# Cross-attention with routed experts on one core: the order of input loads, output weights and expert matrices on one DMA queue

## The chip, the core and the metric

One core of a Trainium2 chip runs the whole kernel. The metric is the device time of one execution in microseconds (us). TensorE is called PE in the profile, its weight loads PEld, VectorE DVE, ScalarE ACT, GpSimd POOL, and SyncE, which here only issues DMAs, SP.

## The reference, cut to what matters

There are 32 records of 128 tokens with 256 channels (`x`), each with a context of the same shape (`ctx_1024`).

```python
def _L0_xattn_ref(q, k, v, Wq, bq, Wk, bk, Wv, bv, Wd, bd):   # 16 heads of 16
    query = (q @ Wq.T + bq).reshape(B, -1, H, D)
    key_p = (k @ Wk.T + bk).reshape(B, -1, H, D)
    value = (v @ Wv.T + bv).reshape(B, -1, H, D)
    logits = jnp.einsum('bsid,bsjd->bsij', query, key_p) / jnp.sqrt(jnp.float32(D))
    attn = jax.nn.softmax(logits, axis=-1)          # heads attend to heads, per token
    out = jnp.einsum('bsij,bsjd->bsid', attn, value)
    out = jnp.transpose(out, (0, 2, 1, 3)).reshape(B, -1, O)
    return out @ Wd.T + bd

x = x + _L0_xattn_ref(_layernorm(x, axis=-1), ctx_1024, ctx_1024, ...)
x = x + _L0_ffn_ref(_layernorm(x, axis=-1), ...)
# ffn: gates = softmax(x_red @ wg_n.T) over 8 experts, idx = argmax, scores = max;
#      o = scores * (gelu(x @ W1[idx] + b1[idx]) @ W2[idx] + b2[idx])
```

## The kernel before, in words

**Attention.** A loop over steps t = 0 to 41 runs on every engine; it is a software pipeline written out by hand. In step t, TensorE projects record a = t (`tensor_project`, lines 921, 924 and 1013: key, value, query and gate columns), computes the logits of record t - 6 (line 933), turns the attention of record t - 7 (line 1024), multiplies record w = t - 8 with the output weights (line 977, `wd`), and computes the values of record t - 7 (line 944). In the first 8 steps the projection stands first in the step, from step 8 on it stands behind `wd`. For its first seven steps TensorE also does three idle transposes at the end (`fill`).

**The round trip.** The heads of a token have to be spread over partitions. So two records at a time, keys, queries and values (`qkv`, 768 KB) are stored to a scratch tensor in HBM (line 280) and loaded back in another order (`ql`, two DMAs of 384 KB, line 289). POOL masks what came back into `kx` (line 393) and ACT copies it into `pad` (line 817), both for record z = t - 5.

**Inputs.** `x` comes in pairs of records (256 KB, line 252) into a ring of 14 slots. ACT takes the moments of record t + 2 in step t (`scalar_ahead`, lines 770 and 773); behind them on ACT stand the moments of the attention's result and the copy `oT` (line 837), which `wd` of the next step reads. The transposed inputs `xc` (x and context, 512 KB for two records, line 258) go to a ring of XC = 4 slots in `r1`; POOL permutes the context of record t + 1 in step t (`pool_context`, line 356), TensorE reads both.

**SP's order.** SP issues nearly all DMAs, in program order, on one queue (`sync_attention`). In an odd step t: wait until the records t - 1 and t are ready (`qad`), store them, load `xc` of t + 3; a row store (`sync_row`, line 272); wait until the store has landed and the buffer `ql` is free, issue the two `ql` loads, load `x` of t + 5. In every step also a row store, and the expert matrices that `MATRIX_AT` puts there (16 of 512 KB: eight W1, eight W2; first at step 22, last at step 35). From step 32 on there are four parts of `b2`. `sync_inputs`, ahead of the loop, issues `xc` and `x` of records 2 and 3, then the output weights and bias (`sync_setup_output`: 768 KB in four DMAs), then `x` of 4 and 5.

**Output weights.** `tensor_gate` (lines 1031 and 1034) folds the gate columns into the output weights. It needs `Wd` and `bd_col` and stands behind the projection of record 1. POOL adds the output bias to `x` of record t - 2 (line 402).

**Experts.** While attention still runs, the first 20 records are routed (`vector_early`, steps 27 to 34, on DVE). From step 34 on, slots of 128 tokens gathered by expert go through two matrix products (lines 1086 and 1116). The first slot needs all eight W1 at step 35, the first product with W2 comes in step 37 and needs all eight W2.

Of the kernel before, what the change touches and what calls it, by code (L numbers as in the profile page):

```python
# [4 lines left out]
P = 128  # L5
C = 256
NH = 16
HD = C // NH
NT = 32
# [9 lines left out]
EXT = C + NL  # L19
# [9 lines left out]
NG_ = NH  # L29
W3 = 3 * HD  # L30
XR = 14
XC = 4
CR = 5
RB = 6
YR = 4
# [12 lines left out]
ROUTE = R1 + 7  # L48
SLOTS_AT = {t: (t - FIRST,) for t in range(FIRST, LAST + 1)}
NEXT = LAST + 1 - FIRST  # L50
MATRIX_AT = (22, 24, 26, 27, 28, 29, 30, 31, 32, 32, 33, 33, 34, 34, 35, 35)
B2_IN = 32
B2_PARTS = 4
SHARE = 1
# [1 line left out]
SELR = NH2 + 2  # L56
PIECES = (("oh_a", 1), ("rv_a", 5), ("rv_a", 10), ("rv_a", 13), ("texp_a", 1), ("selk_a", 1), ("taken_a", 1))

SEMS = ("ld_xx ld_cc ld_x0 ld_x1 ld_x2 ld_c0 ld_c1 st_q0 st_q1 ld_q0 ld_q1 st_r0 st_r1 st_r2 st_r3 st_r4 ld_wq ld_wkv ld_wd ld_wo ld_g ld_gr ld_gt ld_b ld_bd "
        "ld_bc ld_w1 ld_w2 ld_b2 filled ident iotas const cp mask4 pad0 nmax gpow ctr0 ctr gmm gate gx gxs "  # L60
        "wqs wTq gsq nr2 wide qq kv kvad qad xb kx pad qk mx lsub exp sm rsm norm tr_a ax0 ax pvo oT wd x2 nb gm gsub "
        "scaled score nm0 va0 va1 ve rs oh cnt rv selr selp selk invmm texp idg ids ig isc yo yb "
# [4 lines left out]
def live(t):  # L67
    return 0 <= t < NT
# [6 lines left out]
def build(nc, x, xc, wkvT, wqT, wdT, Wd, bkvq, bd, bd_col, w_redT, wgT_in, wg, W1b, W2, b2, out):  # L75
# [7 lines left out]
    with es:  # L83
        def sb(name, shape, dt=f32):
            return es.enter_context(nc.sbuf_tensor(name, shape, dt))
# [43 lines left out]
        rsm = sb("rsm", [P, NH])  # L129
        oT = sb("oT", [P, KC, P])  # L130
        cat = [sb(f"cat{k}", [P, ROW + 1]) for k in range(CR)]
        junk = sb("junk", [P, 2, C])
        nm = sb("nm", [P, 1])
        va = sb("va", [P, 2])
        ve = sb("ve", [P, 2])
# [25 lines left out]
        nr2, nrm, nri = (sb(n, [P, NE]) for n in ("nr2", "nrm", "nri"))  # L161
        warm = sb("warm", [P, 2])
        r0 = sb("r0", [P, 3800])[:, :]
        r1 = sb("r1", [P, 2 * W1W + C])[:, :]
        xcT = r1[:, 0:XC * 4 * P].rearrange("p (n a c) -> p n a c", n=XC, a=4)

        oh = sb("oh", [P, NT, NE], bf16)
# [67 lines left out]
        def sync_setup_output(eng):  # L235
            eng.dma_start(wst, Wd.rearrange("(a p) c -> p a c", p=P)).then_inc(S["ld_wo"], 16)
            eng.dma_start(wD[:, :, 0:C], wdT).then_inc(S["ld_wd"], 16)
            eng.dma_start(bdb[:, 0:C], bd.rearrange("(o n) -> o n", o=1).broadcast_to((P, C))).then_inc(S["ld_bd"], 16)
            eng.dma_start(bdm, bd_col).then_inc(S["ld_bc"], 16)
# [14 lines left out]
        def sync_xc(eng, c):  # L254
            if c < NT:
                if c >= XC:
                    eng.wait_ge(S["qq"], c - XC + 2)
                eng.dma_start(xcT[:, c % XC:c % XC + 2, :, :], xc[c // 2]).then_inc(S[f"ld_c{c // 2 % 2}"], 16)

        def sync_inputs(eng):  # L260
            eng.wait_ge(S["ld_xx"], 16)
            sync_xc(eng, 2)
            sync_x(eng, 2)
            eng.wait_ge(S["ld_x0"], 16)
            sync_setup_output(eng)
            sync_x(eng, 4)

        def sync_row(eng, g):
# [5 lines left out]
        def sync_attention(eng):  # L274
            sync_inputs(eng)
            for t in range(LAST + 2):
                p = t // 2
                if live(t) and t % 2 == 1:
                    eng.wait_ge(S["qad"], t + 1)
                    eng.dma_start(qkv_scr[p], qkv[p % 2][:, :, :, :]).then_inc(S[f"st_q{p % 2}"], 16)  # L280
                    sync_xc(eng, t + 3)
                sync_row(eng, t - 10)
                if live(t) and t % 2 == 1:
                    eng.wait_ge(S[f"st_q{p % 2}"], (p // 2 + 1) * 16)
                    if p > 1:
                        eng.wait_ge(S["kx"], t - 3)
                        eng.wait_ge(S["pad"], t - 3)
                    for h in range(2):
                        eng.dma_start(ql[p % 2][64 * h:64 * (h + 1), :, :, :],
                                      qkv_scr[p].rearrange("(h c g) x w d -> h x c g (w d)", h=2, c=NC_)[h]  # L290
                                      ).then_inc(S[f"ld_q{p % 2}"], 16)
                    sync_x(eng, t + 5)
                for m in range(2 * NE):
                    if MATRIX_AT[m] == t:
                        expert(eng, m)
                m = t - B2_IN
                if 0 <= m < B2_PARTS:
                    if m == 0:
                        eng.wait_ge(S["gxs"], 1)
                    h = NE * C // B2_PARTS  # L300
                    eng.dma_start(b2b[:, m * h:(m + 1) * h], b2.rearrange("e c -> (e c)").rearrange("(o n) -> o n", o=1)
                                  [:, m * h:(m + 1) * h].broadcast_to((P, h))).then_inc(S["ld_b2"], 16)
# [44 lines left out]
        def pool_context(eng, a):  # L347
            if live(a):
                if a == 0:
                    eng.wait_ge(S["ld_cc"], 16)  # L350
                else:
                    eng.wait_ge(S[f"ld_c{a // 2 % 2}"], (a // 4 + 1) * 16)
                if a > 1:
                    eng.wait_ge(S["kv"], a - 1)
                for k in range(KC):
                    i_ = eng.tensor_copy(cp[a % 2][:, k, :].rearrange("p (e c h g) -> p e c h g", e=2, c=NC_, h=2),
                                         xcT[:, a % XC, KC + k, :].rearrange("p (h c e g) -> p e c h g", e=2, c=NC_, h=2))
                i_.then_inc(S["cp"], 1)

        def pool_attention(eng):  # L360
            for t in range(-1, LAST + 1):
                n, v, w, d, z = t + 1, t - 2, t - 8, t - 9, t - 5
                if t == -1:
                    pool_norm(eng)
                    pool_context(eng, 0)
# [172 lines left out]
        def vector_attention(eng):  # L538
            for t in range(LAST + 1):
                a, s0, s1, w = t, t - 6, t - 7, t - 8  # L540
                if t < 7:
                    vector_kv(eng, a)
                    vector_q(eng, a)
                if a == 1:
                    eng.wait_ge(S["gx"], 1)
                    eng.wait_ge(S["ld_bd"], 16)
                    eng.tensor_copy(bdb[:, C:EXT], bY[:, 304:304 + NL])
                    eng.tensor_copy(wD[:, :, C:EXT], bY[:, 320:320 + KC * NL].rearrange("p (a e) -> p a e", a=KC)
                                    ).then_inc(S["gxs"], 1)
# [12 lines left out]
                if live(w):  # L562
# [7 lines left out]
                    if w > 0:  # L570
                        eng.wait_ge(S["gsub"], w)
                    eng.tensor_reduce(gm[:, :], cat[w % CR][:, C:C + NE], AX, ALU.max,
                                      negate=True).then_inc(S["gm"], 1)
                if live(a) and t >= 7:
                    vector_kv(eng, a)
                if ROUTE <= t < ROUTE + 7:
                    vector_early(eng, t - ROUTE)
                if live(a) and t >= 7:
                    vector_q(eng, a)
                if live(s0) and t >= STEADY:  # L580
                    normed(eng, s0)
# [184 lines left out]
        def moments(eng, k, w, in_):  # L766
            if k + (0, 10)[w] > 0:
                eng.wait_ge(S["rs"], k + (0, 10)[w])
            if w == 0:
                eng.activation(junk[:, 0, :], in_, ACT.Identity, scale=-1.0 / C,  # L770
                               accum_out=nm[:, :]).then_inc(S["nm0"], 1)
                eng.wait_ge(S["nm0"], k + 1)
            eng.activation(junk[:, w, :], in_, ACT.Square, bias=nm[:, :] if w == 0 else cat[k % CR][:, EXT - 1:EXT],
                           accum_out=va[:, 1 - w:2 - w]).then_inc(S[f"va{w}"], 1)

        def scalar_ahead(eng, t):
# [136 lines left out]
        def tensor_kv(eng, a):  # L913
            if a > 0:
                eng.wait_ge(S["kvad"], a)
                eng.wait_ge(S[f"ld_c{a // 2 % 2}"], (a // 4 + 1) * 16)
            else:
                eng.wait_ge(S["ld_wkv"], 16)
                eng.wait_ge(S["ld_cc"], 16)
            for k in range(KC):  # L920
                eng.matmul(bKV[:, 0:C], xcT[:, a % XC, KC + k, :], wT[:, k, 0:C], start=(k == 0), stop=(k == KC - 1))  # L921
            eng.wait_ge(S["cp"], a + 1)
            for k in range(KC):
                i_ = eng.matmul(bKV[:, C:2 * C], cp[a % 2][:, k, :], wT[:, k, C:2 * C], start=(k == 0),  # L924
                                stop=(k == KC - 1))
            i_.then_inc(S["kv"], 1)
# [23 lines left out]
        def tensor_attention(eng):  # L950
            for t in range(LAST + 1):
                a, s0, s1, w = t, t - 6, t - 7, t - 8
                if t < 8:
                    tensor_project(eng, a)
                if live(s0):
                    eng.wait_ge(S["kx"], s0 + 1)
# [12 lines left out]
                if live(w):  # L969
# [6 lines left out]
                    for k in range(KC):  # L976
                        i_ = eng.matmul(bY[:, 0:EXT], oT[:, k, :], wD[:, k, :], start=(k == 0), stop=(k == KC - 1))  # L977
                    i_.then_inc(S["wd"], 1)
                if live(a) and t >= 8:
                    tensor_project(eng, a)  # L980
                if live(s1):
                    eng.wait_ge(S["ax"], s1 + 1)
# [13 lines left out]
                for s in slots:  # L996
                    if s != 1:
                        tensor_rows(eng, s)
                if t < 7:
                    fill(eng, 3, bA)  # L1000
                if t == NT + 8:
                    tensor_counts(eng)

        def tensor_project(eng, a):
            tensor_kv(eng, a)
            if a > 0:
                eng.wait_ge(S["qad"], a)
            else:
                tensor_weights(eng)
                eng.wait_ge(S["gate"], 1)  # L1010
                eng.wait_ge(S["wTq"], 1)
            for k in range(KC):
                i_ = eng.matmul(bQ[:, 0:EXT], xcT[:, a % XC, k, :], wT[:, k, 2 * C:3 * C + NL], start=(k == 0),  # L1013
                                stop=(k == KC - 1))
            i_.then_inc(S["qq"], 1)
            if a == 1:
                tensor_gate(eng)

        def tensor_turn(eng, t, s1):
# [194 lines left out]
```

## Time and profile before

| | us |
|---|---|
| median of 3 runs (374.09 to 376.0) | 374.12 |
| the profiled execution's own time | 376.52 |
| its span | 374.7 |
| PE busy | 339.7 (91%) |
| DVE busy | 255.8 (68%) |
| POOL busy | 275.0 (73%) |
| ACT busy | 203.7 (54%) |
| DMA moved | 63.90 MB |

The profile cuts the span into 40 slices of 9.4 us. The slices up to 206 us are the attention; the rest is the experts' slots, in which TensorE is busy nearly throughout. Times below are microseconds from the span's start.

### The profile page before, as it was taken

What the parts mean: (1) busy time and instruction counts of PE and PEld (TensorE: products, weight loads), DVE (VectorE), ACT (ScalarE), POOL (GpSimd) and SP (SyncE); (2) the same over time, 40 slices, a digit from 0 to 9 for tenths busy, and PEclk for the clock granted to TensorE, in tenths of its full rate; (3) what the DMA queues carried; (4) which work ended last, traced back from release to release, by engine and by line L of the source; (5) the groups of instructions that cost most, each with busy time, mean ns of one, the idle gap of its engine ahead of it and who ended that gap; (6) DMA issues with size and microseconds to landing.
All of it is one profiled execution on the core that took longest, in us unless ns stands there. A gap on an engine that the chain in (4) does not pass through costs nothing.

```text
span 374.7 us, 11126 instructions
## 1 busy us (share of the span) xinstructions
PE 339.7 (91%) x3755; PEld 290.5 (78%) x3755; DVE 255.8 (68%) x629; ACT 203.7 (54%) x625; POOL 275.0 (73%) x539
## 2 busy tenths in 40 slices
PE   7898599999999998895767997899999999999994
PEld 6786488888878776674645785789999999999993
DVE  6343788989888885899777656784565556565552
ACT  2334668877787866676663646612443434343431
POOL 4758858987889876777978377672777777778763
PEclk9999699999999999899588999997999999999999
DMA  6899989999999999989798011410122222222210
GB/s 230 268 266 270 225 189 241 253 264 265 247 275 282 293 221 256 299 268 270 189 383 309 16 43 59 132 59 27 62 72 69 75 62 77 62 74 60 62 48 0
DMA packets 55414, 63.90 MB, mean 171 GB/s; under 512 B 36558, under 2 KB 45919, under 8 KB 55360
## 3 DMA queue, kind: packets, MB, share of 16 engines
q1 hardware_dynamic: 50832, 52.78, 49.8%
q0 software_dynamic: 3744, 9.55, 8.5%
q10 hardware_dynamic: 784, 0.87, 0.7%
q8 instruction: 31, 0.51, 0.6%
q14 instruction: 23, 0.19, 0.2%
HBM read 42.02 MB, written 22.09 MB: 171 GB/s over the span
## 4 chain that ended last, share of the span: by engine, by line
PE 61%; DMA 13%; DVE 10%; issue 6%; ACT 5%; POOL 3%; SPq 1%; ACTq 1%; DVEq 1%; POOLq 0%
PE bQ L1116 17%; PE bKV L1086 9%; PE bL L1086 9%; DMA xt<-in_x 7%; PE bY L977 5%; PE bKV L921 3%; PE bKV L924 3%; PE bO L944 3%; PE bQ L1013 3%; DMA qkv_scr<-qkv 3%; PE bL L933 3%; PE bT L1098 2%; DMA r<-row_scr,ig 2%; ACT pad L817 1%; PE bA L1024 1%
## 5 line engine op out<-in xcount | busy, mean ns | idle before, releaser
L1116 PE MATMUL bQ<-w,wA 128*128 x312 | 75.0, 384 | 3.0 <-DVE r L756 2.3
L1116 PEld LDWEIGHTS bQ<-w,wA 128*128 128x128 f32 x312 | 56.8, 192 | 10.6 <-issue 4.4
L393 POOL TENSOR_TENSOR x<-ql,mask 128x1024 f32<-128x1024 f32 x32 | 60.6, 1892 | 0.4 <-DVE texp L638 0.4
L423 POOL DMA_INDIRECT out<-r,isc x39 | 40.8, 1046 | 21.7 <-issue 13.9
L446 POOL DMA_INDIRECT r<-row_scr,ig x39 | 41.8, 1071 | 6.1 <-issue 2.2
L884 ACT ACTIVATE wA<-bL,r 128x128 f32<-128x128 f32 x76 | 21.7, 368 | 40.8 <-PE bL L1086 40.8
L884 ACT ACTIVATE wA<-bKV,r 128x128 f32<-128x128 f32 x80 | 22.8, 367 | 35.2 <-PE bKV L1086 35.2
L1086 PEld LDWEIGHTS bKV<-wA,r 128*128 128x128 f32 x320 | 38.5, 192 | 3.6 <-issue 1.8
L1086 PE MATMUL bKV<-wA,r 128*128 128x128 f32 x320 | 39.4, 276 | 2.0 <-DVE wA L745 2.0
L977 PE MATMUL bY<-wD,oT 128*128 128x265 f32 x128 | 39.7, 437 | 1.2 <-ACT oT L837 1.1
L817 ACT ACTIVATE pad<-ql 64x512 f32<-64x512 f32 x64 | 39.8, 622 | 0.4
L1086 PEld LDWEIGHTS bL<-wA,r 128*128 128x128 f32 x304 | 38.4, 199 | 1.6 <-ACT wA L884 0.6
L1086 PE MATMUL bL<-wA,r 128*128 128x128 f32 x304 | 38.8, 283 | 0.0
L756 DVE TENSOR_TENSOR r<-bQ,b2b 128x256 f32<-128x256 f32 x39 | 16.5, 424 | 32.4 <-PE bQ L1116 32.4
L736 DVE TENSOR_SCALAR r<-w1b 128x1028 f32 x39 | 28.5, 732 | 12.9 <-issue 11.6
L921 PE MATMUL bKV<-wA,r 128*128 128x256 f32 x128 | 33.5, 384 | 1.4 <-DMA r<-in_xc 0.9
L944 PEld LDWEIGHTS bO<-ax,pad 128*32 128x32 f32 x1024 | 16.9, 115 | 22.9 <-ACT ax L863 13.7
L1013 PE MATMUL bQ<-wA,r 128*128 128x265 f32 x128 | 33.9, 387 | 0.3 <-DVE wA L479 0.3
L373 POOL TENSOR_TENSOR cat<-ve,half 128x2 f32<-128x2 f32 x42 | 30.8, 733 | 3.5
L924 PE MATMUL bKV<-wA,cp 128*128 128x256 f32 x128 | 33.0, 380 | 0.0
L808 ACT ACTIVATE bX<-bL 128x256 f32<-128x256 f32 x32 | 11.8, 368 | 37.4 <-DVE bL L554 37.4
L944 PE MATMUL bO<-ax,pad 128*32 128x64 f32 x1024 | 22.3, 231 | 10.4 <-ACT ax L863 10.4
(179 smaller groups left out, 694.0 us busy)
## 6 DMA issues: line engine op xcount, KB each, us to landing
qkv_scr<-qkv SPq DMA_DIRECT2D x16, 768.0 KB, 5.1
ql<-qkv_scr SPq DMA_DIRECT2D x32, 384.0 KB, 5.6
r<-in_xc SPq DMA_DIRECT2D x15, 512.0 KB
row_scr<-cat SPq DMA_DIRECT2D x32, 134.0 KB, 5.6
w1b<-in_W1b SPq DMA_DIRECT2D x8, 514.0 KB, 6.0
w<-in_W SPq DMA_DIRECT2D x8, 512.0 KB, 9.7
xt<-in_x SPq DMA_DIRECT2D x15, 256.0 KB, 6.2
b2b<-in_b SPq DMA_DIRECT2D x4, 256.0 KB, 10.9
```

The lines of the kernel that those rows point to most:

```text
L393: eng.tensor_tensor(quarter(kx[:, z % 2, :]), spread(ql[z // 2 % 2][:, :, z % 2, 0:HD]), mask_k, ALU.mult).then_inc(S["kx"], 1)
L423: eng.indirect_dma_start(out, bass.IndirectOffsetOnAxis(ap=isc[k][:, :], axis=0), yo[k], None, bounds_check=NTOK - 1, oob_is_err=False).th ...
L446: eng.indirect_dma_start(gr[k], None, row_scr[0:R1 * P] if a < S1 else row_scr, bass.IndirectOffsetOnAxis(ap=ig[k][:, :], axis=0)).then_in ...
L817: i_ = eng.activation(pad[n, z % 3, :].rearrange("p (k g h d) -> p k g h d", k=2, g=NG_, h=2) [:, :, :, h, :], ql[z // 2 % 2][n, :, z % 2, ...
L884: i_ = eng.activation(hT[a % 2][:, k, :], bH[a % 2][:, k * P:(k + 1) * P], ACT.Gelu, bias=w1s[a % 2][:, KC * HID + k:KC * HID + k + 1])
L921: eng.matmul(bKV[:, 0:C], xcT[:, a % XC, KC + k, :], wT[:, k, 0:C], start=(k == 0), stop=(k == KC - 1))
L924: i_ = eng.matmul(bKV[:, C:2 * C], cp[a % 2][:, k, :], wT[:, k, C:2 * C], start=(k == 0), stop=(k == KC - 1))
L944: i_ = eng.matmul(out_[32 * r:32 * (r + 1), m * P + q * 64:m * P + (q + 1) * 64], stat[:, 32 * g:32 * (g + 1)], moving[:, (8 * m + 2 * r + ...
L977: i_ = eng.matmul(bY[:, 0:EXT], oT[:, k, :], wD[:, k, :], start=(k == 0), stop=(k == KC - 1))
L1013: i_ = eng.matmul(bQ[:, 0:EXT], xcT[:, a % XC, k, :], wT[:, k, 2 * C:3 * C + NL], start=(k == 0), stop=(k == KC - 1))
L1086: i_ = eng.matmul(bH[a % 2][:, k * P:(k + 1) * P], w1s[a % 2][:, c * HID + k * P:c * HID + (k + 1) * P], gT[a % 2][:, c, :], start=(c == 0 ...
L1116: i_ = eng.matmul(bQ[:, 0:C], hT[b % 2][:, k, :], w2[:, bass.ds(eb * (KH * C) + k * C, C)], start=(k == 0), stop=(k == KH - 1))
```

## The change

The first rows of `MATRIX_AT` move from step 22 to step 27 and the matrices come closer together. `XC` becomes 6, with a third semaphore for the loads; from step 5 on `xc` of t + 5 is loaded behind the `ql` loads and `x`, where `xc` of t + 3 was loaded ahead of the wait for the store. In the first steps `x` stands behind the store instead of behind the `ql` loads. The output weights move from ahead of the loop to SP's step 2, `tensor_gate` from behind projection 1 to behind projection 4, DVE's part of it from step 1 to step 5. The projection stands first in the step for nine steps instead of eight (DVE: eight instead of seven). POOL's bias addition moves from record t - 2 to record t - 6. The `fill` of the first seven steps goes. ACT's unused outputs go to a part of `b2b` instead of `junk`, and the `b2` loads wait for the last of them.

```diff
-XC = 4
+XC = 6
-MATRIX_AT = (22, 24, 26, 27, 28, 29, 30, 31, 32, 32, 33, 33, 34, 34, 35, 35)
+MATRIX_AT = (27, 28, 28, 29, 29, 30, 30, 31, 31, 32, 32, 33, 33, 34, 34, 35)
...
-        r1 = sb("r1", [P, 2 * W1W + C])[:, :]
+        r1 = sb("r1", [P, XC * 4 * P])[:, :]
...
-                eng.dma_start(xcT[:, c % XC:c % XC + 2, :, :], xc[c // 2]).then_inc(S[f"ld_c{c // 2 % 2}"], 16)
+                eng.dma_start(xcT[:, c % XC:c % XC + 2, :, :], xc[c // 2]).then_inc(S[f"ld_c{c // 2 % 3}"], 16)
 
         def sync_inputs(eng):
             eng.wait_ge(S["ld_xx"], 16)
             sync_xc(eng, 2)
             sync_x(eng, 2)
             eng.wait_ge(S["ld_x0"], 16)
-            sync_setup_output(eng)
             sync_x(eng, 4)
...
                     eng.wait_ge(S["qad"], t + 1)
                     eng.dma_start(qkv_scr[p], qkv[p % 2][:, :, :, :]).then_inc(S[f"st_q{p % 2}"], 16)
-                    sync_xc(eng, t + 3)
+                    if t < 4:
+                        sync_xc(eng, t + 3)
+                    if t < 8:
+                        sync_x(eng, t + 5)
+                if t == 2:
+                    sync_setup_output(eng)
                 sync_row(eng, t - 10)
                 if live(t) and t % 2 == 1:
                     eng.wait_ge(S[f"st_q{p % 2}"], (p // 2 + 1) * 16)
...
-                    sync_x(eng, t + 5)
+                    if t > 8:
+                        sync_x(eng, t + 5)
+                    if t > 4:
+                        sync_xc(eng, t + 5)
+                if t == 4:
+                    sync_xc(eng, 8)
...
                     if m == 0:
                         eng.wait_ge(S["gxs"], 1)
+                        eng.wait_ge(S["va0"], NT)
...
-                n, v, w, d, z = t + 1, t - 2, t - 8, t - 9, t - 5
+                n, v, w, d, z = t + 1, t - 6, t - 8, t - 9, t - 5
...
-                if t < 7:
+                if t < 8:
                     vector_kv(eng, a)
                     vector_q(eng, a)
-                if a == 1:
+                if a == 5:
                     eng.wait_ge(S["gx"], 1)
...
-                if t < 8:
+                if t < 9:
                     tensor_project(eng, a)
...
-                if live(a) and t >= 8:
+                if live(a) and t >= 9:
                     tensor_project(eng, a)
...
-                if t < 7:
-                    fill(eng, 3, bA)
...
-            if a == 1:
+            if a == 4:
                 tensor_gate(eng)
```

## Rows read from the trace of the kernel before

**Rows 1.** Stretches: busy us by engine, TensorE's clock, DMA share, GB/s.
```profile
65.10:75.10 10.00, 10.00 (x178) 8.14 (x167) 8.85 (x22) 8.05 (x27) 8.68 (x16) 1.00 0.98 255
125.60:136.40 10.80, 10.25 (x167) 8.21 (x167) 8.85 (x22) 8.41 (x28) 8.88 (x17) 1.00 0.89 272
```

**Rows 2.** TensorE in order of time: `wd` of records 1, 12, 13, 21, 22.
```profile
50.53 1.07 PE L977 MATMUL bY<-wD,oT 128*128 128x265 f32 x4
...
105.73 1.11 PE L977 MATMUL bY<-wD,oT 128*128 128x265 f32 x4
...
111.11 1.13 PE L977 MATMUL bY<-wD,oT 128*128 128x265 f32 x4 [0.25 <-ACT oT L837]
...
156.68 1.98 PE L977 MATMUL bY<-wD,oT 128*128 128x265 f32 x4
...
162.85 1.07 PE L977 MATMUL bY<-wD,oT 128*128 128x265 f32 x4
```

**Rows 3.** SP in order of time: `ql` loads, two stores.
```profile
59.12 1.26 SPq L289 DMA_DIRECT2D ql<-qkv_scr  x2
...
69.62 1.26 SPq L289 DMA_DIRECT2D ql<-qkv_scr  x2
...
100.97 1.25 SPq L289 DMA_DIRECT2D ql<-qkv_scr  x2
...
120.96 1.25 SPq L289 DMA_DIRECT2D ql<-qkv_scr  x2
...
150.81 0.32 SPq L280 DMA_DIRECT2D qkv_scr<-qkv  x1
...
155.65 2.02 SPq L289 DMA_DIRECT2D ql<-qkv_scr  x2
...
163.30 0.32 SPq L280 DMA_DIRECT2D qkv_scr<-qkv  x1
...
168.36 1.25 SPq L289 DMA_DIRECT2D ql<-qkv_scr  x2
...
180.49 2.18 SPq L289 DMA_DIRECT2D ql<-qkv_scr  x2
```

**Rows 4.** DMA view, 97 to 107 us, slices of 0.25 us.
```profile
DMA  9999999999999941000305298999999999999999
GB/s 479 398 369 319 393 393 369 369 385 418 401 418 361 360 141 63 33 16 21 91 4 34 75 180 244 255 260 195 211 201 209 232 221 186 183 217 185 190 202 223
```

**Rows 5.** Chain that ended last: `x` of records 22, 23.
```profile
102.66 6.38 DMA xt<-in_x
```

**Rows 6.** Waits between 105 and 206 us: total, times, longest.
```profile
POOL cp L356 <- DMA r<-in_xc: 4.5, 4, 1.7
```

**Rows 7.** Order of time: routing, `kx` of record 30, W1, W2.
```profile
149.28 0.33 DVE L604 SCALAR_TENSOR_TENSOR r<-glog,io_e 128x160 f32<-128x160 f32 x1 [2.52 <-POOL glog L405]
...
191.77 1.89 POOL L393 TENSOR_TENSOR x<-ql,mask 128x1024 f32<-128x1024 f32 x1
...
194.94 0.70 DVE L736 TENSOR_SCALAR r<-w1b 128x1028 f32 x1 [0.94 <-issue]
...
210.11 1.99 PE L1116 MATMUL bQ<-w,wA 128*128 x8 [0.39 <-issue]
```

**Rows 8.** DMA view, 185 to 205 us, slices of 0.5 us.
```profile
DMA  9999999999989999999999999999999999986318
```

**Rows 9.** SP's queue in order of time, 19 to 24 us.
```profile
19.59 2.13 SPq L289 DMA_DIRECT2D ql<-qkv_scr  x2
21.76 0.67 SPq L252 DMA_DIRECT2D xt<-in_x  x1
23.72 0.33 SPq L280 DMA_DIRECT2D qkv_scr<-qkv  x1
```

**Rows 10.** Waits of 20 to 50 us as in rows 6.
```profile
ACT junk L770 <- DMA xt<-in_x: 9.2, 2, 4.8
```

**Rows 11.** The columns of rows 1 for the stretch 40 to 42 us.
```profile
40.00:42.00 2.00, 0.00 (x0) 0.00 (x0) 1.93 (x5) 1.73 (x4) 2.00 (x2) 0.50 1.16 230
```

More of the change, by code:

```diff
@@ L57 @@
 PIECES = (("oh_a", 1), ("rv_a", 5), ("rv_a", 10), ("rv_a", 13), ("texp_a", 1), ("selk_a", 1), ("taken_a", 1))
-SEMS = ("ld_xx ld_cc ld_x0 ld_x1 ld_x2 ld_c0 ld_c1 st_q0 st_q1 ld_q0 ld_q1 st_r0 st_r1 st_r2 st_r3 st_r4 ld_wq ld_wkv ld_wd ld_wo ld_g ld_gr ld_gt ld_b ld_bd "
+SEMS = ("ld_xx ld_cc ld_x0 ld_x1 ld_x2 ld_c0 ld_c1 ld_c2 st_q0 st_q1 ld_q0 ld_q1 st_r0 st_r1 st_r2 st_r3 st_r4 ld_wq ld_wkv ld_wd ld_wo ld_g ld_gr ld_gt ld_b ld_bd "
         "ld_bc ld_w1 ld_w2 ld_b2 filled ident iotas const cp mask4 pad0 nmax gpow ctr0 ctr gmm gate gx gxs "
@@ L131, in build @@
         cat = [sb(f"cat{k}", [P, ROW + 1]) for k in range(CR)]
-        junk = sb("junk", [P, 2, C])
+        junk = sb("junk", [P, 1, C])
         nm = sb("nm", [P, 1])
@@ L351, in pool_context @@
                 else:
-                    eng.wait_ge(S[f"ld_c{a // 2 % 2}"], (a // 4 + 1) * 16)
+                    eng.wait_ge(S[f"ld_c{a // 2 % 3}"], (a // 6 + 1) * 16)
                 if a > 1:
@@ L573, in vector_attention @@
                                       negate=True).then_inc(S["gm"], 1)
-                if live(a) and t >= 7:
+                if live(a) and t >= 8:
                     vector_kv(eng, a)
@@ L577, in vector_attention @@
                     vector_early(eng, t - ROUTE)
-                if live(a) and t >= 7:
+                if live(a) and t >= 8:
                     vector_q(eng, a)
@@ L769, in moments @@
             if w == 0:
-                eng.activation(junk[:, 0, :], in_, ACT.Identity, scale=-1.0 / C,
+                eng.activation(b2b[:, 6 * C:7 * C], in_, ACT.Identity, scale=-1.0 / C,
                                accum_out=nm[:, :]).then_inc(S["nm0"], 1)
                 eng.wait_ge(S["nm0"], k + 1)
-            eng.activation(junk[:, w, :], in_, ACT.Square, bias=nm[:, :] if w == 0 else cat[k % CR][:, EXT - 1:EXT],
+            eng.activation(junk[:, 0, :] if w == 1 else b2b[:, 6 * C:7 * C], in_, ACT.Square, bias=nm[:, :] if w == 0 else cat[k % CR][:, EXT - 1:EXT],
                            accum_out=va[:, 1 - w:2 - w]).then_inc(S[f"va{w}"], 1)
@@ L915, in tensor_kv @@
                 eng.wait_ge(S["kvad"], a)
-                eng.wait_ge(S[f"ld_c{a // 2 % 2}"], (a // 4 + 1) * 16)
+                eng.wait_ge(S[f"ld_c{a // 2 % 3}"], (a // 6 + 1) * 16)
             else:
```

## The prediction

> **What bounds the kernel now.** I read the page first: TensorE is busy 91% of the span, so the first guess is that only TensorE counts. Its strip of slices says otherwise for the attention: DMA stands at 9 tenths there too, and the two have to be taken apart. The table of stretches does it [rows 1]: from 65.1 to 75.1 us, two steps, TensorE is busy 10.00 of 10.00 us and the DMA engines 0.98. The attention has two bounds that lie almost on one another. The next view is TensorE in order of time, to see which of them gives way: `wd` of records 1 to 12 comes every (105.73 - 50.53) / 11 = 5.02 us, and then ten steps take 105.73 to 162.85 = 57.1 us, 6.9 us more than ten such steps [rows 2]. In front of the first late one, record 13, TensorE waits for ACT's `oT`; the chain of waits leads from there to the load of `x` for records 22 and 23, issued at 102.66 us and landed 6.38 us later [rows 5]. Later POOL waits four times for `xc`, 4.5 us in all [rows 6], and so is late with `kx`, and DVE waits 2.52 us for POOL when routing begins [rows 7]. So once the pipeline is full DMA is what runs late.
>
> How DMA comes to be late is seen on SP's queue [rows 3]. The time at which the `ql` loads are issued (the store has landed) goes 69.62, ..., 120.96: five pairs in 51.34 us, 10.27 us a pair, where TensorE needs 10.04 (two steps). The queue's own period is a little longer than TensorE's. The DMA view of one pair shows what the period is made of [rows 4]: all engines full until 100.5 us (store, then `xc` at 370 to 420 GB/s), then a lull of about 2 us, then 180 to 260 GB/s with the scattered `ql` loads. The lull ends 1.7 us after SP issued those loads at 100.97 us. It is the round trip through SP: the store lands, SP wakes, the loads start. The next store can't help, because SP issues in order. What fills part of that round trip today is `xc`, issued directly behind the store.
>
> **The change part by part.**
>
> *`xc` behind the `ql` loads (ring of six).* From step 5 on nothing but a row store (134 KB) is queued between a store and its `ql` loads. The 512 KB of `xc` no longer run while SP waits, they run behind `x` and ahead of the next store. At the 370 to 420 GB/s of [rows 4] they take 0.52 MB / 0.39 = 1.3 us, and the lull grows by the same. Period after: 10.27 + 1.3 = 11.55 us. Bounds: 10.27 if the store lands earlier by all that `xc` took, 12.1 if `xc` costs its share with ramps (1.8). For the lower end there is a row: the store of step 29, with only a row store behind it since `xc` has ended, is seen landed after 168.36 - 163.30 = 5.06 us, that of step 27, with `xc` behind it, after 155.65 - 150.81 = 4.84 us [rows 3]. No gain from an emptier queue, so I take the full 1.3. The Trainium skill, page "DMA: Bandwidth & Descriptors", section "Latency and other measured facts", says that a lighter load on HBM makes the fixed cost of a DMA smaller. By that rule the lull would shrink and the loss with it; the two stores just named speak against it here, so it only feeds a rival below.
>
> What it buys: `xc` is ready two steps sooner and POOL's waits for it go (the 4.5 us of [rows 6]). But `x` keeps its place behind `ql` and its three steps of lead, and `x` is as late as `xc`: its load is the last to land at record 13, before any matrix. With a longer period `x` decides alone.
>
> *Output weights in step 2.* SP issues the first `ql` loads at 19.59 us and is through at 21.7; `x` takes it to 22.4, and the second store goes out at 23.72 [rows 9]. Now four DMAs stand there (0.67 us for one [rows 9], some 2.2 to 2.6 in all): the store goes out at about 24, as before, but with 768 KB ahead of it in the queue instead of the 256 KB of `x`. 0.52 MB more at 0.2 to 0.4 MB per us is 1.3 to 2.6 us. From there the queue is full, since the stores are ready early: I take +2.5 us for the store of step 9 (bounds 0 and +4). TensorE reaches `tensor_gate` at about 24 us and waits for `bd_col` until about 28.5; it has this time, because `ql` and `xc` of the next pair come no earlier. On the other side the loads of `x` move ahead, which takes away ACT's waits of 9.2 us in all [rows 10], and with them most of the time at 40 to 42 us in which TensorE does nothing [rows 11]. On TensorE the head is even, -1 to +2; what is left of it is the queue's delay.
>
> *Matrices from step 27.* Three leave the pairs of steps 21 to 26, at some 1.4 us each (0.53 MB at 0.38). They were already in the measured times of those pairs. Nine instead of five now stand in steps 27 to 31.
>
> *The rest* costs nothing: the bias addition of POOL keeps its 0.7 us and is needed only at `wd`; `junk` changes its address; the added wait of `b2` is for a moment of step 29, with `b2` in SP's step 32 and nothing behind it that is due; the ninth early projection and DVE's order concern one step. The removed fills free about 0.3 us a step in a stretch that waits for DMA anyway.
>
> **The sum.** I follow L, the time at which SP issues the `ql` loads. Before: 59.12 at step 9, 155.65 at step 27, 168.36 at 29, 180.49 at 31 [rows 3]. After: 59.12 + 2.5 = 61.6 at step 9. Eight periods of 11.55 give 154.0 at step 25. `x` of records 30 and 31 lands 8.1 us behind L (100.97 to 102.66 + 6.38 = 109.04 [rows 3, 5]), at 162.1, and `wd` two steps on starts 2.1 us later (109.04 to 111.11 [rows 2, 5]): record 21 at 164.2 against 156.68, +7.5. At step 27 L is 165.6. Then `x` and `xc` are gone: a period of 10.27 - 1.0 (`x`) = 9.3, plus three matrices 4.2 = 13.5, then plus four, 5.6, = 14.9: L = 179.1 and 194.0 at step 31, +13.5 on 180.49. This has slack on the other side. The last `ql` lands some 6 us behind, at 200; `kx` of record 30 stood at 191.77 [rows 7] and moves to 200: +8.2. The same DMAs as before follow (one W1, eight W2, `b2`): they ended at about 204.3 [rows 8] and end at 217.8, against a first product with W2 at 210.11 [rows 7]: +7.7. The last W1, two matrices behind `ql`, lands at about 201.5 against its first use at 194.94 [rows 7]: +6.5. The three ends and the +7.5 of record 21 agree on +6.5 to +8.2, since each end had 5 to 6 us of slack. From this I take off 0.7 us: the wait of 2.52 us at the start of routing [rows 7] was partly due to POOL's wait for `xc`. Everything behind is TensorE's work in a fixed order and keeps its length. Forecast: +7 us. The profiled execution took 376.52 us with a span of 374.7; the timed runs have a median of 374.12, 2.4 below. On the median: 381.
>
> **The rivals.**
>
> *Faster: the late transfers go and the period does not grow.* The mechanism is the one the step of the matrices has for it: without them in steps 22 to 26 and with `xc` two steps ahead, the 6.9 us of lateness between records 12 and 22 [rows 2] vanish up to routing's own share, estimated at 1.4. Price: -5.5 us, 368.6. It decides where the lull shrinks by 1.0 us or more, so that the period stays under 10.5. For it: with matrices in the queue a pair takes 10.8 us [rows 1], and POOL's waits are real [rows 6]. Against it: the two stores of [rows 3], and the lateness of `x` at 109 us with no matrix yet issued. 0.14.
>
> *Nothing: loss and gain cancel.* With a period of 10.65 L stands at 61.6 + 9 x 10.65 = 157.5 at step 27 against 155.65 [rows 3], which the slack of the tail swallows: 373 to 376. This is also where the skill's rule on lighter load ends if it holds halfway. 0.08.
>
> *Part of it: 376 to 378.5.* The period grows by 0.9, or the head brings no delay: 2.5 to 5 us off L at step 27. 0.12.
>
> *Clock.* From 40 to 42 us TensorE had stood and its clock was at 0.50, the lower level of 1.2 GHz [rows 11]. In the new kernel it stands about 4 us before `tensor_gate` without fills, and some 1.5 us in each of eight pairs. If it spends a third of each pair at the lower level, 10.04 us of TensorE's work take 10.04 / (1 - 1/6) = 12.0, and with part of the wait on top the pair takes 12.4 instead of 11.55: 8 x 0.85 = 7 more, +14, 388. The Trainium skill, page "TensorE: Matmul & The Clock Gate", section "HAM oscillation — how this bites in real kernels", describes just this pattern, a DMA wait in every tile after which the clock is low, and advises to reorder so that the waits go. Against it: waits of under 1 us left the clock at 1.00 at 125 to 136 us [rows 1]. 0.08.
>
> The forecast itself, 378.5 to 385: 0.58.
>
> **How the numbers follow.** What can be told from no change is 0.5%, 372.2 to 376.0. Slower by more: 0.58 + 0.12 + 0.08 = 0.78. Within: 0.08. Faster: 0.14. The range leaves the faster case out and a part of the clock's: 373 to 389.
>
> **What would show it.** In the profile after: `ql` loads issued every 11.3 to 11.8 us from step 9 to 25; a lull in the DMA view of 3 us instead of 2 between store and `ql`; ACT waiting for `x` in most pairs, over 8 us in all, TensorE behind it for `oT`; no wait of POOL for `xc`; `tensor_gate` waiting for `bd_col` until about 28 us; W2 landed after 215 us. The forecast is wrong if the `ql` loads keep 10.3 us or less.

## The result and the profile after

The changed kernel takes a median of 388.91 us (387.53 to 391.42, four runs) against 374.11 us (370.32 to 376.0, four runs) for the kernel before: ratio 1.0441, 95% interval 1.0387 to 1.0494, 14.8 us slower. The forecast was 7 us slower. Ratios leave disturbed runs out, so that one need not be the quotient of two medians. The profiled execution took 389.88 us with a span of 388.1.

The loads of `ql` in the kernel after, in the order of SP's queue (start, length, line, transfer), at steps 9, 17, 25, 27, 29 and 31:

```profile
65.67 1.25 SPq L293 DMA_DIRECT2D ql<-qkv_scr  x2
...
112.21 1.25 SPq L293 DMA_DIRECT2D ql<-qkv_scr  x2
...
158.72 1.85 SPq L293 DMA_DIRECT2D ql<-qkv_scr  x2
...
169.58 1.28 SPq L293 DMA_DIRECT2D ql<-qkv_scr  x2
...
182.97 1.25 SPq L293 DMA_DIRECT2D ql<-qkv_scr  x2
...
197.94 1.63 SPq L293 DMA_DIRECT2D ql<-qkv_scr  x2
```

Eight pairs in 158.72 - 65.67 = 93.05 us are 11.63 us a pair, where the forecast had 11.55 and the kernel before, over the five pairs of steps 11 to 21, 10.27 [rows 3] (the kernel after over the same five: 11.53). But the stretch begins 6.55 us later than before (59.12), and 4.1 us later than the forecast's 61.6. Step 31 is at 197.94 where the forecast had 194.0, 3.9 us later: about the same 4 us are in it.

TensorE in order of time, kernel after: the wait at `tensor_gate`, two early projections, two waits for `ax`, and `wd` of records 1 and 13 (in brackets the wait before it and who ended it):

```profile
28.66 0.95 PE L1039 MATMUL bY<-wA,b2b 128*128 128x9 f32 x4 [4.38 <-DMA b2b<-in_bd_col]
...
31.16 2.05 PE L931 MATMUL bKV<-wA,r 128*128 128x256 f32 x4
...
36.06 1.02 PE L931 MATMUL bKV<-wA,r 128*128 128x256 f32 x4
...
46.09 1.08 PE L954 MATMUL bO<-ax,pad 128*32 128x64 f32 x32 [2.90 <-ACT ax L873]
...
54.70 0.65 PE L954 MATMUL bO<-ax,pad 128*32 128x64 f32 x32 [1.81 <-ACT ax L873]
...
56.58 2.10 PE L987 MATMUL bY<-wD,oT 128*128 128x265 f32 x4 [0.41 <-ACT oT L847]
...
123.12 1.13 PE L987 MATMUL bY<-wD,oT 128*128 128x265 f32 x4 [3.18 <-ACT oT L847]
```

`wd(1)` stands at 56.58 against 50.53, record 13 at 123.12 against 111.11 [rows 2]. So TensorE is 6 us late before the steady stretch begins. The forecast had called TensorE "even" in the head, the first steps in which the pipeline fills. The wait of 4.38 us was foreseen; what it leaves behind was not. Stretches of the kernel after, columns as in [rows 1], the gate's wait, the time behind it, and the ones behind the two waits for `ax`:

```profile
24.50:28.60 4.10, 0.00 (x0) 0.00 (x0) 0.38 (x2) 2.25 (x6) 0.77 (x2) 1.00 1.12 344
28.90:35.70 6.80, 6.80 (x23) 5.87 (x23) 0.69 (x1) 0.36 (x2) 3.72 (x8) 0.51 0.99 250
46.00:49.40 3.40, 3.31 (x38) 2.76 (x39) 0.09 (x1) 0.42 (x2) 1.13 (x2) 0.52 1.12 296
56.20:59.60 3.40, 3.02 (x7) 2.44 (x8) 3.19 (x10) 2.67 (x8) 3.11 (x6) 0.52 1.25 240
```

and the second of these stretches in the kernel before:

```profile
28.90:35.70 6.80, 5.91 (x59) 4.71 (x58) 2.67 (x7) 2.26 (x6) 5.55 (x10) 1.00 0.95 215
```

After the wait TensorE is busy without a gap, but the granted clock is 0.51, the lower level of 1.2 GHz, and the same product takes 2.05 us at 31.16 and 1.02 at 36.06. (The counts 23 and 59 are not a measure of the loss: before, 32 of the 59 products were the narrow ones of the first logits.) The kernel before had such a stretch too, only one and shorter: from 39.7 to 46.3 us its clock was 0.50, with 3.98 us of work in it. In the kernel after the three rows above hold 6.80 + 3.31 + 3.02 = 13.1 us of work at the lower level. Work at half clock takes twice its time, so the difference, (13.1 - 3.98) / 2 = 4.6 us, is an estimate of what the clock costs in the head. The Trainium skill, page "TensorE: Matmul & The Clock Gate", section "HAM oscillation — how this bites in real kernels", describes a low clock behind a DMA wait; the trace agrees here. DVE has hardly anything to do in the stretch behind the gate (0.69 us busy), and its longest wait for TensorE among the logits is a little later, for the logits of record 2, which on TensorE now stand behind the ninth early projection:

```profile
51.69 0.42 DVE L562 TENSOR_REDUCE mx<-bL 128x16 f32<-128x256 f32 x1 [5.59 <-PE bL L943]
```

Waits of the kernel after between 50 and 220 us (who waits for what: total us, times, longest), which answer to [rows 6]:

```profile
PE bY L987 <- ACT oT L847: 7.9, 7, 3.2
ACT b2b L780 <- DMA xt<-in_x: 6.6, 4, 3.1
DVE cat L577 <- DMA row_scr<-cat: 2.5, 1, 2.5
```

POOL's waits for `xc` are gone from the view between 50 and 220 us. Those of ACT for `x` with TensorE behind them stand in their place. The DMA view of the kernel after between 99 and 111 us, slices of 0.3 us, which answers to [rows 4]:

```profile
DMA  8840000002798999999999999999999999999762
```

Six slices at zero and eight (2.4 us) under five tenths, where the kernel before had 2.0 us under five tenths [rows 4]. One lull is not like the next, so I counted the time under five tenths within 4 us of each of the nine `ql` loads of steps 9 to 25, in slices of 0.2 us: 1.4 us on average before, 3.0 after. Last the end of the attention, in the chain that ended last of the kernel after (start, length, what):

```profile
187.43 10.49 DMA qkv_scr<-qkv
197.94 0.54 SPq L293
...
200.97 8.04 DMA row_scr<-cat
209.13 0.45 DVE cat L577
...
210.76 1.62 POOL r L456
...
221.37 0.30 ACT gsc L868
221.69 1.28 ACT L894
223.50 0.64 ACT wA L894 x2
224.13 0.24 issue
224.37 1.77 PE bQ L1124 x7
```

The store of step 31 goes out behind four expert matrices and is seen landed after 10.49 us; those of steps 27 and 29 took 4.84 and 5.06 before [rows 3], and that of step 31 took 5.62. The row store behind it takes 8.04 us, DVE's `cat` has to wait for its slot, POOL's gathers follow, and the first product with W2 starts at 224.37 against 210.11 [rows 7]. What released it is ACT, at the end of this chain, and not the load of W2.

### The profile page after: what moved, and what is told of

It is laid out like the page before. It is cut to its first block, busy times and chain, and to the rows that moved or that the text cites. A ratio compares the mean times of both kernels' runs of the same rounds, so it can differ in the third digit from the quotient of the medians.

```text
span 388.1 us, 11085 instructions
## 1 busy us (share of the span) xinstructions
PE 344.9 (89%) x3734; PEld 293.3 (76%) x3734; DVE 255.7 (66%) x629; ACT 204.0 (53%) x625; POOL 274.6 (71%) x539
## 4 chain that ended last, share of the span: by engine, by line
PE 55%; DMA 18%; DVE 11%; issue 4%; POOL 4%; ACT 3%; SPq 3%; DVEq 1%; ACTq 0%; POOLq 0%
PE bQ L1124 16%; DMA qkv_scr<-qkv 10%; PE bKV L1094 8%; PE bL L1094 8%; DMA xt<-in_x 5%; PE bKV L931 4%; PE bKV L934 4%; PE bQ L1021 3%; PE bY L987 3%; DMA row_scr<-cat 2%; PE bT L1106 2%; PE bO L954 2%; SPq L293 2%; PE bL L943 1%; DMA b2b<-in_bd_col 1%
## 5 line engine op out<-in xcount | busy, mean ns | idle before, releaser
L987 PE MATMUL bY<-wD,oT 128*128 128x265 f32 x128 | 38.8, 429 | 7.9 <-ACT oT L847 7.9
L1094 PEld LDWEIGHTS bKV<-wA,r 128*128 128x128 f32 x320 | 39.4, 196 | 3.7 <-issue 2.0
L1094 PE MATMUL bKV<-wA,r 128*128 128x128 f32 x320 | 40.3, 280 | 2.0 <-DVE wA L755 2.0
L535 DVE TENSOR_TENSOR qkv<-bKV,bqkv 128x512 f32<-128x512 f32 x32 | 22.1, 691 | 24.0 <-PE bKV L934 24.0
L931 PE MATMUL bKV<-wA,r 128*128 128x256 f32 x128 | 37.2, 417 | 0.5 <-DMA wA<-in_wkvT 0.5
L934 PE MATMUL bKV<-wA,cp 128*128 128x256 f32 x128 | 35.9, 406 | 1.0 <-POOL cp L366 0.9
L1021 PE MATMUL bQ<-wA,r 128*128 128x265 f32 x128 | 34.8, 395 | 0.3 <-DVE wA L489 0.3
L987 PEld LDWEIGHTS bY<-wD,oT 128*128 128x128 f32 x128 | 23.9, 207 | 12.9 <-issue 9.8
```

The costliest lines, as they stand in the source:

```text
L1094: i_ = eng.matmul(bH[a % 2][:, k * P:(k + 1) * P], w1s[a % 2][:, c * HID + k * P:c * HID + (k + 1) * P], gT[a % 2][:, c, :], start=(c == 0 ...
```

## The experiments

The theory after the result has two causes. The queue: `xc` out of the lull (the time in which the DMA engines idle while SP waits for the store) makes each pair longer. The head: output weights behind the first `ql` loads, the gate's wait and the clock behind it. The rivals: the matrices now crowded into steps 27 to 35, the removed fills, and the ninth early projection. Times are given as differences to the kernel before on the same chip (medians 374.9, 375.07 and 374.84 us in the three groups of runs); the change as it is stands at +14.8, beside its own 374.11. A difference between two such differences is good to 2 or 3 us only, as the intervals of the ratios show.

**`xc` back in the lull.** The changed kernel with one call moved from behind the `ql` loads to directly behind the store (ahead of SP's wait for it):

```
                     if t < 8:
                         sync_x(eng, t + 5)
+                    if t > 4:
+                        sync_xc(eng, t + 5)
...
-                    if t > 4:
-                        sync_xc(eng, t + 5)
```

> The changed kernel (388.9 us) with one edit: from step 5 on the load of xc stands directly behind the store, ahead of SP's wait for it, and no longer behind the ql loads; ring, head and matrices stay. Theory Q (the 512 KB of xc that no longer fill SP's round trip cost 1.3 us in every pair): the ql loads come every 10.3 us instead of 11.6, the head's 6 to 7 us stay, 381 to 383 us. Rival H (the head and TensorE's clock made it all, the queue only follows): 387 to 389 us, and the ql loads stay 11 us or more apart.

Measured: 379.44 us, +4.5; ratio 1.0101 (1.0055 to 1.0148), 1.6 us under the lower end of what I expected. So 14.8 - 4.5 = 10.3 us of the loss hang on the place of one load. The `ql` loads of steps 9 and 25 in this kernel:

```profile
66.44 2.69 SPq L295 DMA_DIRECT2D ql<-qkv_scr  x2
...
150.38 1.86 SPq L295 DMA_DIRECT2D ql<-qkv_scr  x2
```

10.49 us a pair, 1.14 less than 11.63, and the lull, counted as above, is 1.5 us on average instead of 3.0. The start at step 9 is as late as it was (66.44 against 65.67). The period is the queue's order, the late start something else.

**The head back.** The changed kernel with the output weights ahead of the loop and the gate behind the second projection:

```
+            sync_setup_output(eng)
             sync_x(eng, 4)
...
-                if t == 2:
-                    sync_setup_output(eng)
...
-            if a == 4:
+            if a == 1:
                 tensor_gate(eng)
```

(DVE's reading of the gate goes back to `a == 1` too.)

> The changed kernel with the output weights loaded ahead of the loop again and tensor_gate behind projection 1; xc stays behind the ql loads. Both causes of their own (head 6.5 us, queue 7 us): no 4.4 us wait at tensor_gate, ql loads of step 9 at 59 to 60 us instead of 65.7, then 11.6 us apart, 381 to 384 us. Rival: the queue alone would have made the whole loss, whatever the head does: 387 or more. Rival H: below 377 us.

Measured: 387.34 us (383.14 to 389.51), but ratio 1.0234 (1.0114 to 1.0353), which on 374.9 us is +8.8; the interval is wide. The head is worth between 2 and 10 us by this ratio, and by the median hardly anything (1.6 us under the changed kernel), so its price is taken from the pair with `xc` mended, below. The profiled execution (389.46 us) shows that the edit does not bring back the old head there. `ql` of step 9 is at 64.39, where 59 to 60 was expected, and TensorE has changed one wait for another:

```profile
32.02 2.04 PE L930 MATMUL bKV<-wA,r 128*128 128x256 f32 x4 [3.50 <-DMA r<-in_xc]
...
64.39 1.25 SPq L292 DMA_DIRECT2D ql<-qkv_scr  x2
```

It now waits 3.50 us for `xc`, and the product behind the wait takes 2.04 us, as behind the gate. (In the kernel with both edits, below, the same wait is 1.8 us.)

**Only `xc`.** The kernel before with a ring of six and `xc(t+5)` behind `ql` and `x`, with what the ring brings along (its third semaphore, the load of `xc` for record 8 in step 4, the new address of ACT's unused outputs and `b2`'s wait for them), nothing else of the change:

```
-XC = 4
+XC = 6
...
                     sync_x(eng, t + 5)
+                    if t > 4:
+                        sync_xc(eng, t + 5)
```

> The kernel before with only the place of xc and the ring changed (xc of t + 5 behind the ql loads and x, six slots, from step 5 on); output weights, fills, projections, x, matrices as before. Theory Q: ql loads 11.6 us apart from step 9 to 21 and 12 to 13 with the matrices among them, 382 to 386 us. If six slots and the earlier xc were worth something by themselves: under 377 us.

Measured: 385.58 us, +10.7; ratio 1.0256 (1.0163 to 1.0349). The `ql` loads of steps 9 and 21:

```profile
63.12 1.25 SPq L290 DMA_DIRECT2D ql<-qkv_scr  x2
...
132.80 1.25 SPq L290 DMA_DIRECT2D ql<-qkv_scr  x2
```

Six pairs at 11.61 us, with a lull of 2.9 us on average. Added alone or taken away alone, the move has the same price, 10 to 11 us. The `ql` load of step 9 is 4.0 us later than before (59.12) though the head was not touched; 1.9 us of that were there at step 1 already (21.51 against 19.59 [rows 9]), so up to 2 us of a late start can come from `xc`, which leaves its place at step 5 and not only at step 9.

**Only the matrices.** The kernel before with the new list of steps:

```
-MATRIX_AT = (22, 24, 26, 27, 28, 29, 30, 31, 32, 32, 33, 33, 34, 34, 35, 35)
+MATRIX_AT = (27, 28, 28, 29, 29, 30, 30, 31, 31, 32, 32, 33, 33, 34, 34, 35)
```

> The kernel before with only MATRIX_AT changed to the steps from 27 on. The queue's reading: the pairs of steps 21 to 26 come down to about 10.4 us, those of 27 to 30 grow by 1.5 to 3, the slack of the tail takes most of it: 371 to 374 us. The rival of the prediction (the late transfers were the matrices' doing): 368 to 370 us. If the crowd behind step 27 decides: over 376 us.

Measured: 373.13 us, -1.8; ratio 0.994 (0.9893 to 0.9988). The rival of the matrices falls: this edit alone costs nothing and gains a little at most.

**`xc` and head together.** The edits of the first two kernels in one.

> The changed kernel with both edits: xc directly behind the store, and output weights and tensor_gate at their old places. Nine early projections, no fills, early x, matrices from 27 stay. If the wait at tensor_gate was the head's loss: wd of record 0 near 45 us and 371 to 374 us. If it is the ninth projection and the lost clock (record 0's wd stood at 50.6 us with the weights back): wd of record 0 near 50 us, 376 to 379 us.

Measured: 375.18 us, +0.1; ratio 1.0014 (0.9966 to 1.0061). Behind the mended queue the head is worth 4.5 - 0.1 = 4.4 us. `wd(0)` stands at 47.30, against 53.24 in the kernel with `xc` alone mended and 44.67 before: it lies between the two values expected. What is left over in the head are these waits, between 20 and 55 us:

```profile
PE bO L953 <- ACT ax L872: 5.3, 2, 3.5
DVE mx L561 <- PE bL L942: 6.9, 1, 6.9
```

With no wait at the gate TensorE and DVE still wait for each other. The wait of TensorE for the first `ax` is not new (2.70 us before, at 42.32); the second one, and DVE's of 6.9 us, are, and the ninth early projection stands in front of them.

**Eight early projections.** The kernel with both edits, and the early projections of TensorE from nine to eight (DVE's from eight to seven):

```
-                if t < 9:
+                if t < 8:
                     tensor_project(eng, a)
...
-                if live(a) and t >= 9:
+                if live(a) and t >= 8:
                     tensor_project(eng, a)
```

> The kernel of e5_both_back with eight early projections on TensorE and seven on DVE, as before. Theory N (the ninth projection pushes logits, wd and everything behind it back by a projection and leaves TensorE without cover while ax is made): wd of record 0 some 3 to 4 us earlier than in e5, 371 to 375 us. Rival F (the clock, without fills): within 1 us of e5.

Measured: 370.59 us, -4.5; ratio 0.9883 (0.9789 to 0.9977). Of the two waits of TensorE for `ax` one remains, and `wd(0)` stands at 44.13 in the first block below, against 47.30 in the second, of the kernel with both edits:

```profile
PE bO L953 <- ACT ax L872: 2.7, 1, 2.7
...
44.13 1.08 PE L986 MATMUL bY<-wD,oT 128*128 128x265 f32 x4
```

```profile
47.30 1.06 PE L986 MATMUL bY<-wD,oT 128*128 128x265 f32 x4
```

The ninth projection costs 0.1 + 4.5 = 4.6 us, of which 3.2 are seen at `wd(0)`.

**Fills.** The kernel with both edits, and the idle transposes that the change removed:

```
+                if t < 7:
+                    fill(eng, 3, bA)
```

> The kernel of e5_both_back with the three idle transposes at the end of the first seven steps, as before; nine early projections stay. Rival F (their absence lets TensorE's clock fall to its lower level near 30 us): no low stretch between 28 and 38 us and 2 to 3 us less than e5. Theory N: within 1 us of e5, since xc of record 6 is waited for anyway.

Measured: 374.34 us, -0.7; ratio 1.0038 (0.999 to 1.0085), beside 1.0014 without them. No difference that can be told: with the head mended the fills are worth nothing. In the changed kernel itself, behind the gate's wait, they were not tried.

**Both edits, eight and fills.**

> The kernel of e5_both_back with eight early projections and the fills: what is left of the change is the ring of six with xc two steps further ahead, directly behind the store, x behind the store in the first steps, the later bias addition, and the matrices from step 27 on. 370 to 373 us, at or below the kernel before: the good part of the change, if it has one. If the order of x and xc in the head costs by itself: 374 or more.

Measured: 371.35 us, -3.7; ratio 0.9857 (0.9757 to 0.9957), beside 0.9883 without the fills. Again none. Between the two kernels with fills, nine and eight early projections differ by 3.0 us.

**`x` in the lull too.** The kernel with both edits and eight, and in all odd steps `x` directly behind the store, ahead of `xc`:

```
-                    if t < 8:
-                        sync_x(eng, t + 5)
+                    sync_x(eng, t + 5)
...
-                    if t > 8:
-                        sync_x(eng, t + 5)
```

> The kernel of e6_eight with x of t + 5 too issued directly behind the store in every odd step, before SP waits for it. Theory Q the other way round: another 256 KB move into the round trip's lull, the queue's own period falls from 10.3 to about 9.5 us, under TensorE's 10.04, so the ql loads come 10.0 to 10.1 us apart up to step 21 and wd every 5.0 us; at or up to 2 us under e6 (368 to 371 us), since e6's steps are nearly all 5.0 already. Rival (the place behind the store does not matter, only that xc is early): no change in the spacing; or later ql loads, over 372.

Measured: 368.27 us (367.85 to 369.83), -6.6; ratio 0.9851 (0.9792 to 0.991), the lowest median of all and 20 us under the changed kernel. Against the kernel without this edit (0.9883) the gain is within the noise; the spacing is what tells. The `ql` loads of steps 9 and 25:

```profile
58.07 1.25 SPq L293 DMA_DIRECT2D ql<-qkv_scr  x2
...
138.86 1.26 SPq L293 DMA_DIRECT2D ql<-qkv_scr  x2
```

10.10 us a pair, against 10.47 without the edit, where two steps of TensorE are 10.04. Its DMA view between 97 and 107 us, in the slices of [rows 4]:

```profile
DMA  2799966999898979979999999999964399989999
GB/s 49 180 320 365 365 229 279 426 373 369 294 345 209 187 185 207 224 202 226 201 215 260 253 212 219 183 201 183 174 170 112 84 390 377 393 369 418 344 393 369
```

Of the lull of 2 us nothing connected is left: in 10 us three slices of 0.25 us stand below five tenths; on average over the nine pairs the lull is 0.8 us. The same bytes run, and the queue follows TensorE.

**The kernel before, one line moved.** `x` to directly behind `xc`, ahead of SP's wait:

```
                     sync_xc(eng, t + 3)
+                    sync_x(eng, t + 5)
...
-                    sync_x(eng, t + 5)
```

> The kernel before with one line moved: x of t + 5 is issued behind xc, ahead of the wait for the store, in every odd step. Theory Q: ql loads 10.0 to 10.1 us apart to step 21 instead of 10.27, no wait for x at record 13, 370 to 372.5 us. Rival (a longer burst behind the store delays the ql loads by what it holds, a zero sum): 374 to 377 us.

Measured: 371.31 us, -3.5; ratio 0.9928 (0.9889 to 0.9967). The `ql` loads of steps 9 and 21:

```profile
57.64 1.26 SPq L290 DMA_DIRECT2D ql<-qkv_scr  x2
...
117.88 1.26 SPq L290 DMA_DIRECT2D ql<-qkv_scr  x2
```

Six pairs at 10.04 us, against (120.96 - 59.12) / 6 = 10.31 [rows 3], and a lull of 0.8 us on average against 1.4. The rule holds in the other direction: what goes into the lull shortens the pair.

**The changed kernel with the old list of matrices.**

```
-MATRIX_AT = (27, 28, 28, 29, 29, 30, 30, 31, 31, 32, 32, 33, 33, 34, 34, 35)
+MATRIX_AT = (22, 24, 26, 27, 28, 29, 30, 31, 32, 32, 33, 33, 34, 34, 35, 35)
```

> The changed kernel with MATRIX_AT as before (first at step 22). If the queue only adds up: three pairs grow by 1.4 us each and the last two shrink by as much, L at step 31 as in the changed kernel, 387 to 390 us. If the crowd of matrices ahead of the last store (its landing took 10.5 us, and the row store behind it held DVE up for 2.5 us) has a price of its own: 384 to 387 us.

Measured: 389.07 us, +14.2; ratio 1.0395 (1.0327 to 1.0464), as the changed kernel. In the late queue the list makes no difference. This kernel also says something on the end of the attention. DVE does not wait for the row store in it, `ql` of step 31 is issued at 198.46, and the first product with W2 comes all the same at 223.44, 0.9 us earlier than in the changed kernel:

```profile
198.46 2.36 SPq L293 DMA_DIRECT2D ql<-qkv_scr  x2
...
223.44 1.99 PE L1124 MATMUL bQ<-w,wA 128*128 x8
```

**The changed kernel with eight early projections alone.**

> The changed kernel with eight early projections (seven on DVE). With xc in its old place this was worth 4.6 us; here xc stays behind the ql loads. If the queue sets the pace from step 9 on, part of it is swallowed: 385 to 388 us. If head and queue add: 384 us or less.

Measured: 385.61 us, +10.8; ratio 1.0299 (1.0237 to 1.0362): 4.0 us less than the change, where the same edit gave 4.6 behind the mended queue. The late queue swallows little of it.

## Why the prediction was right in sign and too small in size

The prices, each as a step between two neighbouring kernels: `xc` out of the lull 10.3 us, output weights and gate 4.4, ninth projection 4.6. By the ratios in place of the medians they are 12.8, 3.3 and 4.9. The three by the medians sum to 19.3; the kernel without the three stands at -4.5, and 19.3 - 4.5 = 14.8. The sum closes by construction, since each step starts where the last one ends; what supports it is that `xc` moved alone costs as much (+10.7) and that eight projections alone gain nearly as much (4.0). That remainder is close to the matrices alone (-1.8) and `x` earlier (-3.5, from the kernel before in all steps, where the change moves it only up to step 7); this last attribution is argued from size, not shown. POOL's later bias addition was in no experiment undone by itself.

- **The period: right.** 11.55 forecast, 11.63 measured, and 11.61 for `xc` alone. The two stores that were set against the Trainium skill's rule of lighter load (page "DMA: Bandwidth & Descriptors", section "Latency and other measured facts") judged rightly: with less in the queue the lull grew, from 1.4 to 3.0 us on average. Right too were the signs: `xc` without a wait, and ACT late for `x`, though four times and 6.6 us in all where most pairs and over 8 us were forecast. What POOL's freedom is worth by itself no run shows.
- **The failed step: "On TensorE the head is even, -1 to +2; what is left of it is the queue's delay."** `wd(1)` was 6.05 us late and the first `ql` of the steady stretch 6.55, where 2.5 was forecast. The sum took the output weights as bytes in a queue. I had the gate's wait right (4.38 us, until 28.66), and argued that TensorE "has this time". It hadn't: the 6.8 us of work behind the wait ran at half clock, and with the stretches behind the two waits for `ax` 13.1 us of work did, against 3.98 before. The store of step 9 goes out late (62.39 against 55.04) because the projection of record 9 is late on TensorE (58.48 against 51.44; the store follows it by 3.9 and 3.6 us), and not because of bytes in the queue. The credit on the other side did not come either: ACT's waits of 9.2 us for `x` went, but TensorE still stood for the first `ax`, 2.90 us where it had stood 2.70. The clock stood among the rivals, but for every pair at 14 us; it struck the head, and between 60 and 188 us only two stretches of about 4 us, behind 124 and 158 us. How much of the 4.4 us is the gate's wait itself and how much the clock behind it, no experiment separates.
- **The same step, second half: "the ninth early projection and DVE's order concern one step".** A projection that I costed at nothing measured 4.6 us, 4.0 in the change as it is and 3.0 beside the fills. It does stand in one step, but in the head of a pipeline that is not yet full, between TensorE's logits and DVE's softmax, where no other work covers it: DVE waits 5.59 us for the logits behind it (no such wait was over 1.0 us before), and TensorE waits twice for `ax`, 4.7 us in all (once before, 2.70).
- **The 4 us more at step 9 went through to the end**: step 25 at 158.72 against 154.0, step 31 at 197.94 against 194.0. `wd` of record 21 was at 169.42, 12.7 us late, where the forecast had +7.5.
- **The slack of the tail: too large by 3 to 4 us.** I had reckoned each end by its own load and found 5 to 6 us of slack. The forecast's first W2 product was at 210.11 + 7 = 217.1; with L (the `ql` load of step 31) 4 us later it would be at 221.1. It was at 224.37. The chain that ended there is one that no term names: a row store behind the late store of step 31. But this chain is not the whole reason: with the old list of matrices it is gone, and the product still comes at 223.44. Put as a distance, the forecast left 217.1 - 194.0 = 23.1 us between L and the first W2 product. It was 26.4 in the change, 25.0 with the old list, and 24.8 with `xc` moved alone (196.20 to 220.97), the least of all. So the row store and the crowd of matrices account for 1.4 us or so; what holds the other 2 is open. In the kernel with `xc` mended this product stands at 215.58, and with the head back as well at 208.03, under the 210.11 of before.
- **The matrices: as forecast, no great term.** Their own gain is small, and none where the queue is late.
- **The range** (373 to 389) held the median at its very edge. That is luck: its upper end came from the clock's case, in which every pair grows, and not from the head.

The rival of a gain, priced at 368.6, did not come for the change. Its condition was a lull smaller by 1 us. The kernel that comes nearest to it, by putting `x` and `xc` in the lull (0.8 us instead of 1.4), took 368.27; that the numbers meet is chance, since this kernel has other edits too.

## What to carry to other kernels

Where an in-order queue stores, waits and loads back, put other loads between the store and the wait. In this kernel 512 KB on the wrong side cost 1.1 to 1.4 us in each pair, about what their bytes take, and 256 KB more on the right side gave back 0.3 to 0.4, until TensorE's own 10.04 us a pair were the bound. Before a load is moved ahead, ask which wait ends on it, and what happens to the loads it passes. In a pipeline's head, cost every added instruction and every wait twice, at full and at half clock, since little covers them there.

## What the runs showed of the hardware

A wait of 4.38 us of TensorE was followed by 6.8 us at a clock of 0.51, though TensorE was busy without a gap in them; one of 2.90 us was followed by 3.4 us at 0.52. One and the same wait can do either: behind the second one for `ax`, 1.81 us long, `wd(1)` took 2.10 us in the changed kernel and 1.13 in the kernel with `xc` back in the lull. Idle transposes in the early steps made no difference to the time (ratios 1.0038 beside 1.0014, 0.9857 beside 0.9883). A store of 768 KB was seen landed after 4.84 and 5.06 us with one load or a row store behind it and after 10.49 behind four expert matrices; a row store of 134 KB took 8.04 us behind two `ql` loads and two matrices. In these cases the landing followed the bytes ahead of a transfer more than its own.
